# Two attention layers and two expert layers on one core: score products parted, the front of layer 1 reordered, blocks ended without a drain

## The reference

```
x = x + L0_xattn(layernorm(x), ctx, ctx)      # 8 heads of 4 features
x = x + L0_ffn(layernorm(x))                  # 8 experts, top 2, 640 rows each, silu gate, 1024 hidden
x = x + L1_xattn(layernorm(x), ctx)           # 16 heads of 16 features
x = x + L1_ffn(layernorm(x))                  # 15 experts, top 3, plus a shared one, exact gelu gate
```

```
q = query @ Wq + bq;  k, v = split(context @ Wkv + bkv)
scores = einsum('bhid,bhjd->bhij', q, k) * 16 ** -0.5
out = einsum('bhij,bhjd->bhid', softmax(scores), v) @ Wout + bout
```

## Time and profile before

| | us |
|---|---|
| median of 3 runs | 1383.97 |
| profiled execution | 1380.14 |
| its span | 1378.4 |
| TensorE busy (share of span) | 1183.1 (86%) |
| VectorE | 737.0 (53%) |
| ScalarE | 536.8 (39%) |
| GpSimd | 406.3 (29%) |

### The profile page before, as it was taken

The page is one execution under the profiler, slowest core; times in us unless marked ns, Lnnn a source line. Parts: engine busy times, 40 slices in busy tenths (PEclk is TensorE's granted clock), DMA queues, the critical chain, the costliest instruction groups (busy, mean ns, idle before and its releaser), DMA issues. The chain is left out here.

```text
span 1378.4 us, 20546 instructions
## 1 busy us (share of the span) xinstructions
PE 1183.1 (86%) x6794; PEld 771.7 (56%) x6795; DVE 737.0 (53%) x1374; ACT 536.8 (39%) x1096; POOL 406.3 (29%) x443
## 2 busy tenths in 40 slices
PE   4799988279999999998458888889996999999987
PEld 1323334179999999998213334344444755555544
DVE  5567533245665556543356665656625634444447
ACT  2176443043454345432505454455561422322310
POOL 4122354522343224300501112120001146666520
PEclk9688555579999999999658999889997899999999
DMA  3410200142144213300542243221105452222243
GB/s 104 184 47 1 77 29 13 36 144 74 62 131 131 78 55 126 112 20 20 171 133 88 84 129 90 89 70 48 40 1 185 174 206 75 76 76 83 68 139 113
DMA packets 82559, 123.44 MB, mean 90 GB/s; under 512 B 17618, under 2 KB 54953, under 8 KB 82226
## 3 DMA queue, kind: packets, MB, share of 16 engines
q1 hardware_dynamic: 72018, 94.92, 21.3%
q0 software_dynamic: 10464, 27.52, 6.3%
HBM read 89.06 MB, written 35.39 MB: 90 GB/s over the span
## 5 line engine op out<-in xcount | busy, mean ns | idle before, releaser
L1779 DVE TENSOR_REDUCE M<-S 128x2 f32<-128x1024 f32 x128 | 153.8, 1220 | 51.2 <-PE S L1390 39.2
L1675 ACT ACTIVATE PT<-S 128x512 f32<-128x512 f32 x256 | 138.9, 594 | 93.9 <-PE S L1414 85.1
L222 POOL TENSOR_TENSOR w12l<-stage,w12h 128x1024 fp32r<-128x1024 f32 x28 | 67.8, 2421 | 199.8 <-ACT w12h L216 199.8
L2055 PE MATMUL pg<-W,hold 128*128 x248 | 121.0, 610 | 2.9 <-ACT hold L2137 1.2
L1198 DVE TENSOR_TENSOR HTm0l<-HFm,HTm0h 128x320 fp32r<-128x320 f32 x128 | 122.0, 953 | 1.0
L1204 DVE TENSOR_TENSOR HFm<-Um,SGm 128x320 f32<-128x320 f32 x128 | 62.3, 487 | 79.5 <-ACT SGm L1167 79.1
L1167 ACT ACTIVATE SGm<-Gm 128x320 f32<-128x320 f32 x128 | 56.0, 438 | 118.0 <-PE Um L1125 117.2
L910 DVE TENSOR_REDUCE M<-S 128x2 f32<-128x1024 f32 x64 | 77.1, 1222 | 34.0 <-PE S L426 30.1
L1138 PE MATMUL Ym<-w3h,HTm0h 128*128 128x256 f32 x320 | 93.3, 292 | 0.0
L1390 PE MATMUL S<-KS,QS 48*128 48x512 f32 x256 | 71.2, 554 | 25.6 <-issue 9.5
L1427 PE MATMUL PV<-PT,VA 128*32 128x256 f32 x1024 | 87.1, 416 | 5.1 <-issue 3.0
(11 more groups left out here) (273 smaller groups left out, 2502.2 us busy)
## 6 DMA issues: line engine op xcount, KB each, us to landing
stage<-in_W12T SPq DMA_DIRECT2D x32, 512.0 KB
stage<-in_W3T SPq DMA_DIRECT2D x16, 512.0 KB
W<-in_fc1T SPq DMA_DIRECT2D x2, 3840.0 KB, 24.5
KS<-scrk SPq DMA_DIRECT2D x96, 64.0 KB, 2.2
QS<-scrq SPq DMA_DIRECT2D x96, 64.0 KB, 2.2
W<-yk SPq DMA_DIRECT2D x16, 384.0 KB, 7.9
xs<-zeros POOLq DMA_DIRECT2D x10, 512.0 KB, 4.5
XSm<-xs SPq DMA_DIRECT2D x8, 640.0 KB, 4.9
```

Source lines behind the costliest of these rows:

```text
L222: pool.tensor_tensor(ew.part(1, s, c), ew.stage[:, c % STAGES, :], ew.part(0, s, c).bitcast(F32), ALU.subtract).then_inc(ew.low_done, 1)
L1675: act.activation(PT[:, at % SLICES, 2 * hp + j, :], S2[:, j, :], ACT.Exp, scale=HP ** -0.5).then_inc(exp_done, 1)
L1779: dve.tensor_reduce(M[:, n % 3, at:at + 2 * TPB + 1:2 * TPB], out[:, :, :], AX.X, ALU.max).then_inc(S1.done(("max", c)), 1)
L2055: m = pe.matmul(H[:, c % 2, :], XST[:, c % 2, k, :], W1[:, k, bass.ds(e, 1), :], start=(k == 0), stop=(k == KD - 1))
```

## The change

Three edits. Every block is opened with `no_gpsimd_drain=True`: the other engines still drain ahead of the barrier, GpSimd does not, and the barrier is made of semaphores alone. In `layer1`, `scores` does one of its two products per call, and the beat calls it once ahead of the half value product and once behind it. At the front, VectorE does the value rows of batch 0 behind the normalization instead of ahead of the gathered sums, and SP issues the key stack of group 1 in beat -6 (before: -2) and the query stack of group 0 in beat -2 (before: -1), while that of group 1 stays in -1.

```diff
-        block = ctx.enter_context(nc.Block())          # in layer0, experts0, layer1, ffn1
+        block = ctx.enter_context(nc.Block(no_gpsimd_drain=True))
...
-            def scores(s):
+            def scores(s, j):
 
                 n, i = divmod(s, BEATS1)
                 kt, hp = pairs(i)
-                if i == 0:
+                if i == 0 and j == 0:
                     pe.wait_ge(nm_loaded[n % 2], 16 * SHIFT * (n // 2 + 1))
-                for j in range(2):
-                    at = slice(64 * j, 64 * j + 64)
-                    wait(pe, exp_done, 2 * s + j - 1)
-                    pe.matmul(S2[:, j, :], KS[at, n % SLOTS1, hp, kt * P:(kt + 1) * P], QS[at, n % SLOTS1, hp, :],
-                              start=True, stop=True).then_inc(s2_ready, 1)
+                at = slice(64 * j, 64 * j + 64)
+                wait(pe, exp_done, 2 * s + j - 1)
+                pe.matmul(S2[:, j, :], KS[at, n % SLOTS1, hp, kt * P:(kt + 1) * P], QS[at, n % SLOTS1, hp, :],
+                          start=True, stop=True).then_inc(s2_ready, 1)
...
                 if 0 <= s < NC1:
-                    scores(s)
+                    scores(s, 0)
                 if s >= 3 and (s - 3) // 2 < TPB * NG1:
                     values(*divmod((s - 3) // 2, TPB), (s - 3) % 2)
+                if 0 <= s < NC1:
+                    scores(s, 1)
...
                 for n in range(NG1):
-                    if t == max(8 * n - 10, -6):
+                    if t == (max(8 * n - 10, -6) if n != 1 else -6):
                         load_stack("k", n)
-                    if t == (max(8 * n - 9, -1)):
+                    if t == max(8 * n - 9, -2):
                         load_stack("q", n)
...
                 if t == -5:
                     apply(0, 0)
+                    keep_v(0)
...
-                    if name == "v":
+                    if name == "v" and b:
                         keep_v(b)
...
-    with nc.Block() as block:                          # recycle
+    with nc.Block(no_gpsimd_drain=True) as block:
```

More of the change, by code:

```diff
@@ L1053, in experts0 @@
                                     "h_done", "y_ready", "y_done", "y_stored"))
-        block = ctx.enter_context(nc.Block())
+        block = ctx.enter_context(nc.Block(no_gpsimd_drain=True))
         def pairs(eng, expert):
```

## The result

The changed kernel takes 1399.95 us (median of 4 runs, 1390.62 to 1404.1) against 1382.65 us of the kernel before in the same comparison: ratio 1.0117, 95% interval 1.006 to 1.0174. It is slower, by more than the 0.5% that can be told from no change. The forecast was 1381 with a range of 1371 to 1395. Two later comparisons of the same two kernels gave 1.0057 (1.0026 to 1.0089) and 1.013 (1.0098 to 1.0162); so the loss is 8 to 18 us. Ratios and their intervals leave out executions more than 1.5% above the fastest one of the same kernel, medians hold them all. The profiled execution of the changed kernel took 1402.0 us, its span is 1400.3.

A forecast was written before the change was run, and what follows sets the result against it. TensorE was taken as the busiest engine in the first expert layer and layer 1's attention. The terms -3.5 - 3.4 + 4.3 = -2.6 us, put on the median of 1384.0, gave 1381 us, range 1371 to 1395.

The forecast's parts named there:

- The seams: Layer 0's block end and the front of layer 1: shorter stalls, -3.5 and -3.4 us.
- The drain's 3.5 us: End of layer 0's block: without GpSimd's drain the next load and expert layer move up, -3.5 us, bounds -3.5 and 0.
- the front: Front of layer 1: VectorE's new order and SP's earlier stack loads together give -3.4 us.
- the copy: Front of layer 1: ScalarE's copy of the transposed rows starts sooner, -2.2 us, bounds -3.3 and 0.
- the loads: Front of layer 1: earlier stack loads on SP bring the first maxima product forward, -1.2 us, bounds -2 and +0.4.
- The third rival: Block end and front give nothing, +4.3 us remains with up to -2 of the front: 1387 us; chance 0.12.
- The overlap: Main loop: the second score product runs beside the next beat's first maxima product, adding nothing to a plain beat.
- The second rival: Main loop: second score product doesn't run beside the next maxima product, +12.8 us in sum, 1397 us; chance 0.15.
- So half of the 20.0 goes: -10: Main loop: parting the score products halves TensorE's 20.0 us of waits for ScalarE, -10 us, bounds -20 and 0.
- 34 x 0.42 = +14.3: Side-work beats: in 34 of them the second score product runs alone for 0.42 us, +14.3 us, bounds +7 and +21.
- The two together, +4.3: Main loop: -10 from halved waits and +14.3 from lone products make the parting cost +4.3 us.
- The clock: Layer 1's attention: a tenth of 99 us at 1.2 GHz changes level, up to 5 us less or 10 more; chance 0.08.

The follow-up runs named there:

- e5: The kernel before with only the score products parted, without the new front or the drain edit; 1404.25 us, ratio 1.0107.
- after_again: The changed kernel, unaltered, measured again beside its variants against the kernel before; 1393.46 us, ratio 1.0057.
- together_again: The changed kernel with both score products ahead of the half value product again, profiled beside the kernel before; 1375.01 us, ratio 0.9923.
- after_third: The changed kernel, unaltered, measured in a later comparison against the kernel before; 1404.71 us, ratio 1.013.
- together_third: The changed kernel with both score products together again, measured in a later comparison against the kernel before; 1375.19 us, ratio 0.9925.
- e4: The changed kernel with the second score product behind the output's transpose and all side tasks; 1372.71 us, ratio 1.0118 to the kernel before.
- e2: The changed kernel with the score products parted only in beats without side work; 1363.09 us, ratio 1.0039 to the kernel before.
- e3: The changed kernel with the score products parted only in beats with side work; 1373.48 us, ratio 1.0123 to the kernel before.
- f1: The changed kernel with 30 unread products added before the waits for VectorE's rows; 1387.96 us, ratio 1.0031 to the kernel before.

## Why the prediction was wrong

- *The seams*: right. The drain's 3.5 us are gone in every trace without it, and show as -2.9 in this pair only because GpSimd came to the barrier 0.6 us later. At the front it is -4.2 for -3.4; together -7.1 for -6.9, and 690.38 for the forecast 690.6. In the front's own terms, the copy gave 1.9 for 2.2 (680.78 to 675.95, less 2.9), and the loads 2.3 for 1.2, beyond their bound of 2: from the first store to the first maxima product it is now 7.90 us for 10.18, as the product follows the last of the six loads' issue by 1.8 us and not by the assumed 2.8. The two kernels with the new seams and the old score order stand at 0.9923 and 0.9925, and the one on the kinder chip at 0.9955. The third rival, that the seams give nothing, is out.
- *The overlap*: right. The second rival, that it doesn't happen, gave 1397 and so came near the measured time, by a mechanism that isn't there: the products start together at 952.42 and 952.43, and plain beats are shorter than before, not longer. The Trainium skill (TensorEngine Tiling (Array Packing), Key Properties) has a change of mode drain TensorE; between 48-row and 64-row products no such price is in these rows.
- *"So half of the 20.0 goes: -10"*: failed as a reading of its row. The row went to 48.7, since it counts weight loads that wait beside a running value product. In beats what the waits gave is 0.68 us in each eight, some 11 over the 128, so the size came out about right by luck, for a wrong reason.
- *"34 x 0.42 = +14.3"*: in the stretch at full clock the side-work half of eight beats gives back 0.53 us, some 8 over the stage. 0.42 holds for one lone product at full clock; part of it replaced a wait that stood there before. It left out the beats behind the last maxima products, where the second product has no partner: the beats 129 to 140, all at full clock in both, take 19.0 us in the changed kernel and 17.7 in the kernel before, +1.3.
- *The two together, +4.3*: right in size. Without the clock part, four pairs of traces give +7.1 (changed against before), +3.9 (`e5` against before), +3.5 (`after_again` against `together_again`) and +0.4 (`after_third` against `together_third`; about +5 once beats 129 to 140 are priced as measured). Only the last pair is known to share a chip. The 107 beats at full clock give +6.3.
- *The clock*: the step that failed. The sum was made without it, and as a rival it was sized at 5 less or 10 us more from "a tenth" of 99 us. It was a third in the first trace (+35 us) and up to four fifths (+76): by the division +19 to +38 us of time, the last some 33 as measured. In the first pair the spans differ by -7.1 (seams) + 7.1 (parting) + 20.9 (clock) + 1.0 (behind the stage) = 21.9 us, for the forecast -6.9 + 4.3 = -2.6. The chance of 0.08 was too small for a term that no row bounded. What the runs show in its place is this chain: a drop behind a wait, then work at half speed, for longer than before, in which each lone product costs 0.72 at 1.2 GHz (937.40 to 938.12) for 0.42.

What stays open is why the parting lengthens the time at 1.2 GHz. That a wait for VectorE's rows sets off a drop is shown (beats 78 to 83), but those waits are in both kernels. e4 shows that it isn't the added work, e5 that it isn't the front, and e2 and e3 that no one kind of beats carries all of it. For the longest of the low stretches, in beats 121 to 128, it is the beats with side work: 23.9 us in the changed kernel, `after_again`, e5 and e3, 24.7 in `after_third`, 20.5 in e4, and 6.8 in the kernel before, in each kernel with the products together and in e2. In the changed kernel no wait lies in its last 22 us, so it isn't waits within it that keep the level low. But f1 has the same order there and, with three unread products ahead of the row transposes, only 10.2 us. Whether it is that half of the array's rows stand alone for longer in the parted order, or what TensorE did just before, no run here tells apart.

The best kernels found are the two with the seams, the products together and the 30 unread products: 0.9896 with 0.9843 to 0.9948 and 0.9838 to 0.9953. Without the unread products it is 0.9925; that they add something rests on the one short stretch, the intervals overlap.

## What to carry to other kernels

A stage whose granted clock is well below 1 has a second price list: take its time at the low level apart into busy and idle, since half of the busy part is the most that the level can take from the products themselves (here 8.0 us for 25.5 busy in one stretch), and ask of a reordering what it does to that part before counting tenths of a microsecond at full speed. A wait of a weight load is not an idle array: look at what runs beside it. Where an edit has parts, time the kernel without the riskiest one: here two seams worth 0.8% were hidden under a loss of 2%.

## What the runs showed of the hardware

- GpSimd's drain at the end of layer 0's block took 3.51 us, and all of it was on the path: from the last scatter's issue to the next block's first load it is 6.36 to 6.37 us with it and 2.83 to 2.85 without. In the small clearing block a drain took 0.04 us.
- One kernel's stage varies by its clock: that of the changed kernel took 380.5, 373.3 and 390.0 us in three comparisons, with 131, 121 and 172 us at 1.2 GHz, while that of the kernel before took 352.5 and 352.7 with 97 and 90.
- TensorE stayed at 1.2 GHz from 1003.21 to 1025.58 without a gap in its work, 22.4 us, and in another profile of the same kernel through 62 us in which it was busy for 50.7; in the kernel before it was back at 2.4 GHz 6.8 us after the same fall. No rule that I could read from these traces says beforehand which it will be.
- The lower level cost less than half of the time spent at it: 2.5 to 3.1 us for 6.8 in beats 78 to 83, and 8.0 us for 27.0 in beats 129 to 140.
- Products that nobody reads shortened the same stretch by 2.5 to 3.1 us in all five kernels that had them, where they filled a wait of some 3 us.
